# Mixture-of-experts rows in 27 units of 256 instead of 21 units of 384

## What is computed

```python
logits = x @ gate_w.T + gate_b
top_vals, top_idx = jax.lax.top_k(logits, TOP_K)          # TOP_K = 2
routing = jax.nn.softmax(top_vals.astype(jnp.float32), axis=-1)
for e in range(E):                                        # E = 8
    h = x @ w1[e].T + b1[e]                               # 512 -> 1024
    x_glu = h[:, 0::2]
    x_lin = h[:, 1::2]
    y = x_glu * jax.nn.sigmoid(1.702 * x_glu) * (x_lin + 1.0)
    ye = y @ w2[e].T + b2[e]                              # 512 -> 512
    we = jnp.sum(routing * (top_idx == e), axis=-1)
    out = out + ye * we[:, None]
```

## Time and profile before

| | us |
|---|---|
| median of 3 runs (2089.98 to 2098.82) | 2093.15 |
| the profiled execution: its time | 2092.03 |
| the profiled execution: its span | 2090.2 |
| PE busy in the span | 1449.9 |
| DVE busy | 1539.3 |
| ACT busy | 813.4 |
| POOL busy | 657.2 |

### The profile page before, as it was taken

The page is one execution under the profiler, slowest core; times in us unless marked ns, Lnnn a source line. Parts: engine busy times, 40 slices in busy tenths (PEclk is TensorE's granted clock), DMA queues, the critical chain, the costliest instruction groups (busy, mean ns, idle before and its releaser), DMA issues. The chain is left out here.

```text
span 2090.2 us, 28976 instructions
## 1 busy us (share of the span) xinstructions
PE 1449.9 (69%) x9451; PEld 741.8 (35%) x9565; DVE 1539.3 (74%) x2159; ACT 813.4 (39%) x1392; POOL 657.2 (31%) x281
## 2 busy tenths in 40 slices
PE   0041241377389999999999714695699999999970
PEld 0021240133134444444444201245355555555530
DVE  6988959999598888888888387855566666666645
ACT  1022210033147777777777600001344444444410
POOL 8925101156400000000000012210366555566636
PEclk9665555598589999999999955555799999999985
DMA  4000040046522222222223320012466566566628
GB/s 128 0 0 0 0 111 2 0 144 224 175 76 89 88 91 89 86 89 87 91 89 101 124 83 29 26 50 86 156 202 199 195 203 196 192 191 191 191 66 266
DMA packets 152485, 230.34 MB, mean 110 GB/s; under 512 B 22654, under 2 KB 77822, under 8 KB 152394
## 3 DMA queue, kind: packets, MB, share of 16 engines
q1 hardware_dynamic: 142722, 201.47, 29.3%
q0 software_dynamic: 8752, 28.06, 4.8%
q10 hardware_dynamic: 960, 0.17, 0.0%
HBM read 164.25 MB, written 65.08 MB: 110 GB/s over the span
## 5 line engine op out<-in xcount | busy, mean ns | idle before, releaser
L1240 ACT ACTIVATE pT<-p 128x512 f32<-128x512 f32 x800 | 423.2, 608 | 153.2 <-PE p L1141 150.0
L1213 DVE TENSOR_REDUCE mxa<-p 128x1 f32<-128x512 f32 x640 | 410.2, 683 | 96.0 <-PE p L1123 53.9
L1706 POOL TENSOR_TENSOR wl<-shared,wh 128x2048 bf16<-128x2048 f32 x60 | 255.7, 4290 | 127.7 <-ACT wh L1782 127.7
L1141 PE MATMUL p<-qs,ks 128*128 128x512 bf16 x635 | 242.1, 381 | 24.9 <-ACT pT L1240 12.4
L1123 PE MATMUL p<-ks,qs 128*128 128x512 bf16 x564 | 220.3, 393 | 37.3 <-DMA vs<-d_v 32.5
L668 POOL TENSOR_TENSOR xT<-xT,qcbb_ctx 128x2560 f32<-128x2560 f32 x4 | 17.9, 4476 | 703.8 <-DVE qcbb_ctx L686 703.8
L1739 PE MATMUL p<-xh,wh 128*128 128x384 bf16 x672 | 219.7, 327 | 1.2 <-DVE xl L1819 1.2
L1739 PE MATMUL p<-xl,wh 128*128 128x384 bf16 x672 | 219.7, 327 | 0.0
L1739 PE MATMUL p<-xh,wl 128*128 128x384 bf16 x672 | 219.7, 327 | 0.0
L1159 PE MATMUL p<-pT,vs 128*32 128x128 f32 (+1 forms) x2560 | 205.5, 439 | 1.4 <-ACT pT L1240 1.4
L1836 DVE TENSOR_TENSOR yl<-yf,yh 128x384 bf16<-128x384 f32 x84 | 140.8, 1676 | 48.5 <-ACT yh L1797 48.5
(11 more groups left out here) (337 smaller groups left out, 2538.6 us busy)
## 6 DMA issues: line engine op xcount, KB each, us to landing
shared<-in_w1T SPq DMA_DIRECT2D x42, 1024.0 KB
shared<-in_w2T SPq DMA_DIRECT2D x21, 1024.0 KB
d_y<-yo SPq DMA_DIRECT2D x63, 256.0 KB, 4.8
d_v<-xT SPq DMA_DIRECT2D x20, 512.0 KB, 3.9
vs<-d_v SPq DMA_DIRECT2D x32, 320.0 KB
d_o<-osb SPq DMA_DIRECT2D x32, 320.0 KB, 2.2
d_q<-xn SPq DMA_DIRECT2D x16, 480.0 KB, 2.8
d_k<-xn SPq DMA_DIRECT2D x16, 480.0 KB, 2.8
```

The lines of the kernel that those rows point to most:

```text
L1141: mm = pe.matmul(out, ks[u][:, h, k], qs[u][:, h, 0:512], start=True, stop=True)
L1213: dve.tensor_reduce(mxa[u][:, h, qt:qt + 1], bank, AX.X, ALU.max, negate=True).then_inc(s_mfree, 1)
L1240: act.activation(dst, ps[:, second_bank(c, s)], ACT.Exp).then_inc(s_p, 1)
L1706: pool.tensor_tensor(wl[n % 2][:, k], wf[:, k], wh[n % 2][:, k], ALU.subtract).then_inc(s_wl, 1)
```

## The change

One constant is changed:

```diff
-UNIT = 384
+UNIT = 256
 UNITS = (TOK * TOPK - EXP_N) // UNIT + EXP_N
 COLS = UNITS * UNIT // P
```

## The result

Four runs of the changed kernel took 2136.53 us in the median (2135.14 to 2139.11), four of the kernel before, on the same chip, 2092.59 (2089.98 to 2098.82). The ratio is **1.0207, 95% interval 1.0182 to 1.0232**: slower by 2.1%. Forecast were 2137.0 us and 2120 to 2180. The profiled execution of after took 2137.40 us with a span of 2135.6, 45.4 more than that of before; forecast were 44.2.

The account below looks back on a forecast made before the run. A loop of POOL's weight subtractions and PE's short path, nearly level with PE, was taken to bound the kernel; 26 intervals of 21.7 us gave +55.5, less 7.8, 2.0 and 1.5, +44.2: 2137 us, range 2120 to 2180.

Parts of the forecast that it names:

- The loop: Experts stage, from one start of POOL's three subtractions to the next: 25.50 us before, 21.7 us a unit forecast with 256 rows.
- the table above: The loop's terms, forecast against measured, from POOL's subtractions through PE's products to POOL's next start: 21.72 forecast, 21.87 measured.
- The new wait for `xl`: PE's next first products wait for the last `xl`, formerly covered by twelve q = 2 products: 1.20 us, bounds 0 and 1.63.
- The wait for `yl`: PE's wait at line 1750 for `yl`, held back by POOL: to grow from 0.6 to some 2 us a unit.
- The sum: Whole kernel: units +55.5, last unit -7.8, landing of rows -2.0, router -1.5, together +44.2 us.
- router and gathers together: Ahead of the first product: rows' landing -2.0 us (between 0 and -4.1) and router's fewer columns -1.5 us.
- The load: Third weight load: 5.5 us taken, 6.36 left, costed at nothing; rival that it binds, 2179 to 2219 us, chance 0.13.
- The clock: Rival: PE's clock falls to 1.2 GHz in idle gaps; +28 us if a quarter, +113 if always; chance 0.15.
- the 4.3 us of PE work: Loop's t = 3 products, four transposes and 24 first products, 1.31 + 0.43 + 2.60 us, doubled at the lower clock.
- The spacing of matmuls: 24 first products: weight loads hide behind 256 columns, 2.86 us; by the skill page 0.6 us a unit more, 16 in all.
- Faster: Rival: the loop isn't binding, the busiest engine PE sets the unit at 17.0 us; 2014 us, chance 0.03.
- point of decision: Unit distance in the experts stage below which the change wins: 20.0 us.

Follow-up runs that it names:

- experiment 1: Changed kernel (units of 256) plus twelve 512-column products with unused results, behind the transposes of turns 2 and 3: 2165.28 us, 23.07 us a unit.
- (4): Changed kernel with POOL's third subtraction covering half its columns from unit 3 on: 2108.48 us, 20.45 us a unit from there.
- (2): Changed kernel with only two of four tiles of each weight piece loaded from unit 1 on: 2137.57 us, 21.82 us a unit.
- experiment 3: Changed kernel with `yl` made from PSUM instead of `yf`, PE's first products waiting for it: 2111.72 us, 21.1 us a unit.
- 5: Changed kernel with turns 2 and 3 ahead of the t = 3 products and two `xl` ahead of the last `yl`: 2111.87 us, 20.9 us a unit.
- experiment 6: Changed kernel with the edits of 5, and each first cast waiting for its own weight piece only: 2102.72 us, 20.47 us a unit.
- (10): Order of experiment 9 with 256 rows, but all three subtractions on POOL: 2101.70 us, 20.53 us a unit.
- experiment 7: Experiment 6 with the third subtraction on DVE behind the last `xl`: 2103.37 us, ratio to before 1.0061, 20.43 us a unit.
- experiment 9: Experiment 7 with second products t by t, `xh` and `xl` of turns 0 and 1 earlier, biases prepared ahead: 2028.90 us, ratio to before 0.9695.
- experiment 8: Kernel before (units of 384) with the edits of 5, experiment 6 and experiment 7: 2146.98 us, ratio 1.0263, 28.3 us a unit.
- 11: Order of (10) with units of 384, all three subtractions on POOL: 2130.63 us, ratio to before 1.0179, 27.3 us a unit.

## Why the prediction was right, and where its terms were off

**The loop.** 21.7 us a unit were forecast and 21.81 measured, and no term of the table above is off by more than 0.1. That the loop is what binds, and not a set of waits that merely fits the sum, the runs show from three sides: work put into its PE part lengthens the unit by about what exceeds the wait (experiment 1), work taken off POOL shortens it (4), and transfers of half the size leave it as it is (2).

**The new wait for `xl`.** Forecast 1.20 us in each unit; measured 27.8 us in 24 waits, 1.16 each. The dropped products of 2.59 us thus gained some 1.4, and experiment 1, which puts them back, measured 1.26.

**The wait for `yl`** was forecast to grow to some 2 us a unit. It is 74.9 / 25 = 3.0: about 2.1 before the products of t = 2, and 1.45 more before those of t = 3 in the units with a steady clock. The mechanism was right, the second place wasn't counted. It cost nothing, since PE's idle time there isn't on the path.

**The sum.** The intervals between units went from 511.50 to 2054.00 - 1483.93 = 570.07 us, +58.6 for +55.5: 26 times 0.11 is 2.9 of the difference. The ends of the stage, in timelines of PE and POOL of after, to be laid beside the earlier trace rows:

```profile
1479.59 1.12 PE L1724 MATMUL p<-ident,xg 128*128 128x128 f32 x4 [7.85 <-DMA xg<-d_x,slot_token]
```

```profile
2073.77 0.96 POOL L1877 DMA_INDIRECT yg<-d_y,slots  x1 [23.12 <-PEq L1861]
```

The last unit takes 2073.77 - 2054.00 = 19.8 us instead of 27.8, -8.0 for -7.8. The first product comes 4.1 earlier, for 3.5 forecast for router and gathers together; the wait for the landed rows alone fell by 4.6, beyond the 4.1 at the far end of its bounds, while the router's matrix products began 1.4 later in this execution. From the first gather of `combine` to the span's end it is 1.0 us less, which no term had. 58.6 - 8.0 - 4.1 - 1.0 = 45.5, the measured 45.4.

**The load.** I took 5.5 us for a third load, with 6.36 left, and cost it at nothing. Size and cost were both right for this kernel: 5.4 in experiment 1 and after, with 6.5 to the first cast and no wait for it in the record. The choice of 5.5 between 4.96 and 9.50 was an estimate, though, and it doesn't carry over to other orders of work: with gathers and writes issued right beside it the load took 6.3 (experiment 3), and the expectation of that run, made with 5.5, came out 0.7 us a unit too low. So the transfer's leg lies only about 1 us behind the leg through PE, and that is why experiments 3 and 5 gave half of what the PE leg alone would give, and why 6 was needed.

**The clock.** This rival's mechanism happened, its price didn't. From unit 0 on, the records of after have eleven stretches of 3.4 us at the lower level. Windows of after around one:

```profile
1760.87:1763.31 2.44, 0.38 (x3) 0.01 (x1) 2.44 (x2) 0.84 (x2) 2.44 (x2) 1.00 0.96 369
1763.90:1767.30 3.40, 3.40 (x10) 1.22 (x8) 2.93 (x2) 0.95 (x3) 3.27 (x1) 0.50 0.88 286
1767.30:1771.00 3.70, 2.59 (x16) 1.45 (x15) 2.80 (x8) 0.65 (x2) 0.97 (x1) 0.99 0.70 213
```

It falls behind PE's longest wait and is up again when the t = 3 products start. What it slows are the second products of t = 0 to 2, which have 1.45 us of idle time behind them: 3.4 us at half speed lose 1.7, of which 0.1 to 0.2 show. Units with such a stretch took 21.86 us in the mean, the others 21.78. The forecast's price assumed that the slow stretch falls on the 4.3 us of PE work that are on the path. Where less idle time lies behind, the same stretch costs 0.6 us (experiment 6), 1.6 (10) or 1.7 (4). The Trainium skill (TensorE: Matmul & The Clock Gate, section HAM oscillation) is borne out in that the clock falls in a kernel with idle gaps between bursts, but not in every burst: 11 stretches in 27 units, and 2137 us, not 2250. The case from which the Trainium skill has this there waits longer between its bursts than the 2 us here.

**The spacing of matmuls.** In after the first products start every 0.109 us (1770.60, 1770.71), a third less than 0.1625 and within 0.003 of what 256 columns are at 2.4 GHz, each with weights of its own; 24 of them and the latency are 2.89 us for 2.86. The figure that the Trainium skill gives for such a stream (the same page, section Back-to-back issue gap), by which up to 25 ns more would have stood in each, isn't borne out at 256 columns; by it the time would have been some 16 us longer.

**Faster.** The forecast put the point of decision at a unit of 20.0 us. The experiments bear it out from both sides: 20.43 us (7) gives 1.0061, 17.63 (9) gives 0.9695. The reason given against it, that the load of a piece waits for its subtraction, held for this order of work; with the load at its measured 5.4 us instead of 4.96 its lower limit of 20.2 would be 20.6. But it was the limit of this order, not of 256 rows: where the first cast waits for its own piece alone (6), units of 19.97 came out, and with a third of the subtractions on DVE (9) they came to 17.63.

## What stays open

The whole form of experiment 9, split and order, wasn't tried with 384 rows; 8 and 11 each tried a part of it and were slower. That the other part wouldn't have mended them is argued, not shown. Which of the order's three moves gives most at 256 rows wasn't taken apart. What makes the clock fall in one unit and not in the next, the runs don't tell.

## What to carry to other kernels

The size of a tile trades padding against what each tile costs whatever its size; look for the loop that carries that fixed cost from tile to tile, engine by engine, since the busiest engine (here PE, at 97%) may be level with a loop that doesn't shrink. Work that is removed may have been the cover of a wait: price what stood beside it before counting its time as saved. And when two legs of a loop are nearly level, shortening one gives little; measure the second, a transfer above all, under the traffic that it will really meet, and then change both, with an order made for the tile's size.

## What the runs showed of the hardware that I had not expected

- The same 1 MB load doesn't take the same time in every order of work: from issue to landing 5.4 us in the mean with gathers and result writes 2 us or more behind it (experiment 1), 6.3 with them within 0.7 us (experiment 3).
- POOL's indirect gather lasts 2.60 us instead of 0.95 when it is issued while DVE works on a subtraction with two SBUF inputs (experiment 9, the second gather at 1751.65; DVE's subtraction ran from 1751.14 to 1753.43). The same gather takes 2.45 us in experiment 7 and 2.71 in 8, where it meets the same subtraction, and never more than 1.07 in after, where POOL has all three subtractions. What holds it up was not taken apart.
- The same 128 x 2048 subtraction takes 4.07 us on POOL and 2.28 on DVE (experiment 8).
- A single low stretch of the clock was 3.4 us each time, and its price ran from 0.1 to 1.7 us, by how much idle time stood behind it.
